# A memset between row scatters: GpSimd clears a spare tile after each indirect DMA

## The chip, the cores and the metric

The kernel runs on one core of one Trainium2 chip. The metric is the device time of one execution in microseconds (us), as the median over timed runs. The profile of one separate execution, taken by the hardware profiler, gives what the engines did and when.

## The reference

The input is `hidden`, 16 sequences of 512 rows of 256 numbers (8192 rows). Layer one is a memory network trained at test time; layer two is a top-1 mixture of 8 experts.

```
k, v, q = dwconv4(h @ Wk.T), dwconv4(h @ Wv.T), dwconv4(h @ Wq.T)     # 64 columns each
alpha, eta, theta = mean(sigmoid/sigmoid/softplus of h @ aW.T, h @ eW.T, h @ tW.T)
for chunk of 128 rows:
    g = clip(grad of sum((silu(k W1.T) W2.T - v)^2) at the chunk's first W)   # per row
    scan over rows: Sm = eta Sm - theta g;  W = (1 - alpha) W + Sm
    retrieved = silu(q W1.T) W2.T          # with each row's own W
out = rmsnorm(retrieved @ Wo.T) * norm_g * (h @ gW.T + gb)
x = layernorm(h + out)
e = argmax(x @ gate_w.T)                   # one of 8 experts for each row
result = layernorm(x + x @ expert_w[e].T)
```

## The kernel before, in words

The 16 sequences are split into 4 groups (g) of 4, and the 512 rows into 4 chunks (c) of 128, which makes 16 steps (c, g) of layer one. Each step goes through `project`, `respond`, `learn`, `retrieve` and `epilogue`. These are Python generators: each `yield` ends a piece, and the string `ORDER`, written out by hand, says in which order the pieces' instructions are put on the engines' queues. An engine runs its own queue strictly in order; between engines, semaphores decide (`mark` counts an instruction, `wait` waits for a count).

The end of `epilogue` sends the rows of layer one to DRAM, sorted by expert. It computes for each row its place (`where_f`, then `index`, an int32 cast on GpSimd), and then GpSimd issues four indirect DMAs (L1033), one for each sequence of the group: each writes 128 rows of 260 numbers to 128 places of `sorted_rows`. That is 64 scatters in all. They read `rows`, which has two buffers.

The second layer is `experts()`. It works on 36 pairs of tiles of 128 sorted rows (the last pair has one tile, so 71 tiles). For pair t: `load` (SP issues two row loads from `sorted_rows`), `turn` (TensorE transposes, ScalarE copies, L1228), `multiply` (eight TensorE matmuls, L1248, then statistics on VectorE, L1252 to L1261), `scale` (the layernorm's factors, ACT L1267 and DVE L1269 and L1271), `send` (ScalarE writes the normalized rows to `os`, two instructions of L1282; GpSimd scatters them to `out`, one indirect DMA a tile, L1287). There are six load buffers, three transposed ones and four `os` buffers, so `send(t)` on ScalarE waits until the scatter of pair t-4 has landed. Which tile belongs to which expert is worked out by `table` in three parts; the first part needs the scatters of steps 0 to 11, so the expert pairs run partly beside the last four steps of layer one, and the pairs of the last table need all 64 scatters.

What else GpSimd does, in the same queue: small operations of the epilogue (L931, L933 for `rms`, L955 to L960 for `rstd`), of `learn` (L797 to L803, `weight` L812), the loads of the residual (L943), `end_c` (L705), `routed` (L1021) and, in the first 13 steps, wide products (L699, L715, L809, L850). The constructs at L98 (`M.apart`) add one to a semaphore on an engine's sequencer to keep two waits apart.

At the end SP waits until the last scatters have landed (L1307). The program ends there.

Of the kernel before, what the change touches and what calls it, by code (L numbers as in the profile page):

```python
# [27 lines left out]
P = 128  # L28
B = 16
S = 512  # L30
H = 256
# [37 lines left out]
class Counts:  # L69
# [9 lines left out]
    def mark(self, e, name, instruction):  # L79
        instruction.then_inc(self.sem[e], 1)  # L80
        self.count[e] += 1
        self.at[name] = (e, self.count[e])

    def wait(self, e, *names):

        need = {}
        for name in names:
            if int(name.rsplit(".", 1)[1]) >= 0:
                who, n = self.at[name]
                need[who] = max(need.get(who, n), n)  # L90
        for who, n in need.items():
            if self.reached[e, who] < n:
                self.engines[e].wait_ge(self.sem[who], n)
                self.reached[e, who] = n
# [54 lines left out]
def build(nc, dram):  # L149
    out = dram["out"]  # L150
    with ExitStack() as ctx:
# [193 lines left out]
        nc.vector.wait_ge(s_prep, n_bias)  # L345

        layers(nc, ctx, sb, sem, dict(locals()))


def layers(nc, ctx, sb, sem, v):  # L350
# [12 lines left out]
    pe, act, dve, pool, sp = nc.tensor, nc.scalar, nc.vector, nc.gpsimd, nc.sync  # L363
# [3 lines left out]
    def two(name, shape, dt=F32):  # L367
        return [sb(f"{name}{i}", shape, dt) for i in range(2)]
# [65 lines left out]
    where_f = sb("where_f", [P, NB])  # L434
    index = two("index", [P, NB], I32)
    s_scatter = [sem(f"s_scatter{i}") for i in range(2)]

    pro = Slots("pro", banks[0:3], NC * G * 9 + NC * G // 2)
    lrn = Slots("lrn", banks[3:4], NC * G * 4)
# [471 lines left out]
    def epilogue(c, g):  # L911
# [120 lines left out]
        for b in range(NB):  # L1032
            pool.indirect_dma_start(sorted_rows[:, :], bass.IndirectOffsetOnAxis(index[i2][:, b:b + 1], 0), R[:, b, :], None,  # L1033
                                    bounds_check=NE * REGION - 1, oob_is_err=False).then_inc(s_scatter[i2], 16)
        yield

    s_blank = sem("s_blank")
# [144 lines left out]
    def tiles_of(t):  # L1182

        return 1 if t == PAIRS - 1 else 2
# [5 lines left out]
    def moved(t):  # L1190

        return 32 * (t // LOADS) + 16 * tiles_of(t)
# [80 lines left out]
    def send(t):  # L1273

        o = t % ROWS_OUT
        key, both = product[t]
        if t >= ROWS_OUT:
            act.wait_ge(s_out[(t - ROWS_OUT) % LOADS], moved(t - ROWS_OUT))
        wait("act", f"x_shift.{t}")
        for i in range(tiles_of(t)):  # L1280
            mark("act", f"x_os{i}.{t}" if i < tiles_of(t) - 1 else f"x_os.{t}",
                 act.activation(os_[o][:, i, :], both[:, i, :], ACT.Identity, bias=rs[o][:, 2, i:i + 1], scale=rs[o][:, 1, i:i + 1]))  # L1282
        late.freed_by(key, f"x_os.{t}")
        for i in range(tiles_of(t)):
            wait("pool", f"x_os{i}.{t}" if i < tiles_of(t) - 1 else f"x_os.{t}", f"x_tok.{t}")
            M.apart("pool")
            pool.indirect_dma_start(out[:, :], bass.IndirectOffsetOnAxis(xs_token[t % LOADS][:, i:i + 1], 0), os_[o][:, i, :], None,  # L1287
                                    bounds_check=TOK - 1, oob_is_err=False).then_inc(s_out[t % LOADS], 16)

    def experts():  # L1290

        for t in range(PAIRS + 2):
            for stage, lag in ((load, 0), (turn, 0), (scale, 2), (multiply, 1), (send, 2)):
                if 0 <= t - lag < PAIRS:
                    stage(t - lag)
                    yield
# [3 lines left out]
    for letter, stage in dict(p=project, s=respond, l=learn, r=retrieve, e=epilogue).items():  # L1300
        steps.update({f"{letter}{n:x}": stage(n // G, n % G) for n in range(NC * G)})
# [74 lines left out]
```

## Time and profile before

| what | value |
|---|---|
| median of 3 runs | 544.11 us (542.71 to 547.35) |
| the profiled execution: span from first to last instruction | 578.0 us (no other time of this execution is given) |
| TensorE busy | 458.5 us, 79% |
| VectorE busy | 376.7 us, 65% |
| GpSimd busy | 326.8 us, 57% |
| ScalarE busy | 309.7 us, 54% |
| TensorE clock granted, mean | 0.910 of full |

The profiled execution is the longest of the executions told of here: its span is 33.9 us over the median of the timed runs. All rows below are of that execution. Busy shares are averages over stages with different limits. On the page, "L1287" is line 1287 of the kernel; "issue" is idle time in which no wait is visible, and "remote" or "another core or an unknown queue" a wait that ended with a semaphore event for which the profile names no instruction.

### The profile page before, as it was taken

The numbers are of one execution on the slowest core, as the hardware profiler recorded it, in microseconds if no ns is written. First come the engines' busy times: TensorE is split into PE (matmuls) and PEld (weight loads), VectorE is DVE, ScalarE is ACT, GpSimd is POOL, SyncE is SP. The second block draws the span as 40 slices with busy tenths as digits, with TensorE's granted clock in tenths as the row PEclk, the third lists the DMA queues.
The fourth block names the chain that finished last, engine by engine and source line by source line (L and its number), as shares of the span: only waits on it lengthen the run. The fifth ranks groups of instructions, "written<-read, shape, count | busy, mean of one in ns | idle before, by whom it ended". The sixth has DMA issues, their size and how long they took to land.

```text
span 578.0 us, 11149 instructions
## 1 busy us (share of the span) xinstructions
PE 458.5 (79%) x3502; PEld 347.1 (60%) x3502; DVE 376.7 (65%) x1123; ACT 309.7 (54%) x779; POOL 326.8 (57%) x451
## 2 busy tenths in 40 slices
PE   4589889999888998888998898766858774855773
PEld 2356656777665877667675775555646553644662
DVE  3365886898795868769789696777644543333433
ACT  1254375566575485665738656464656553314544
POOL 2004535446748686685757657672477666445466
PEclk9797999999998999998999999885887987768788
DMA  8412352345553536445263545474364644425431
GB/s 228 130 74 61 107 124 71 120 129 101 158 130 96 161 85 164 95 141 135 79 176 74 157 110 151 134 231 110 93 178 133 177 140 137 131 91 161 130 120 43
DMA packets 61354, 73.21 MB, mean 127 GB/s; under 512 B 17293, under 2 KB 48206, under 8 KB 61296
## 3 DMA queue, kind: packets, MB, share of 16 engines
q1 hardware_dynamic: 50624, 46.12, 28.5%
q0 software_dynamic: 8848, 25.44, 16.6%
q10 hardware_dynamic: 1824, 0.93, 0.6%
q8 instruction: 29, 0.48, 0.4%
q14 instruction: 29, 0.24, 0.2%
HBM read 44.19 MB, written 19.22 MB: 110 GB/s over the span
## 4 chain that ended last, share of the span: by engine, by line
PE 41%; DVE 20%; ACT 11%; issue 10%; POOL 8%; another core or an unknown queue 5%; DMA 3%; SPq 1%; ACTq 0%; POOLq 0%; DVEq 0%
DVE kq_in L559 8%; PE bank L518 6%; PE bank L1248 5%; PE bank L605 4%; POOL sorted_rows L1033 3%; PE bank L536 3%; ACT rows L966 2%; PE bank L920 2%; PE both L1248 2%; ACT os L1282 2%; PE bank L686 2%; DVE gt L609 1%; PE both L886 1%; PE bank L1225 1%
## 5 line engine op out<-in xcount | busy, mean ns | idle before, releaser
L1287 POOL DMA_INDIRECT out<-os,xs_token x71 | 70.1, 988 | 46.0 <-ACT os L1282 26.4
L1033 POOL DMA_INDIRECT sorted_rows<-rows,index x64 | 68.7, 1074 | 30.0 <-issue 16.6
L1248 PE MATMUL bank<-shared,front 128*128 x212 | 60.6, 435 | 27.3 <-ACT rs L1267 8.5
L518 PE MATMUL bank<-front 128*64 128x256 f32 x512 | 64.8, 408 | 13.3 <-DMA bias_t<-in_bias_t 7.7
L559 DVE SCALAR_TENSOR_TENSOR kq_in<-shared,conv_w,kq_in 128x256 f32<-128x256 f32 x144 | 69.0, 536 | 9.5 <-ACT kq_in L553 9.3
L605 PE MATMUL bank<-front 128*128 128x256 f32 x256 | 63.1, 396 | 4.8 <-DVE bias_g L324 4.8
L1248 PEld LDWEIGHTS bank<-shared,front 128*128 128x128 f32 x212 | 43.9, 219 | 36.5 <-issue 30.3
L518 PEld LDWEIGHTS bank<-front 128*64 128x64 f32 x512 | 38.8, 148 | 34.4 <-issue 10.8
L605 PEld LDWEIGHTS bank<-front 128*128 128x128 f32 x256 | 48.2, 196 | 12.7 <-issue 6.6
L937 DVE SCALAR_TENSOR_TENSOR y<-bank,rms,gt 128x256 f32<-128x256 f32 x64 | 26.5, 476 | 17.1 <-POOL rms L933 10.2
L1252 DVE BATCH_NORM_STATS2 st<-bank 128x6 f32<-128x256 f32 x53 | 20.2, 421 | 26.3 <-remote 11.9
L927 ACT ACTIVATE junk<-bank 128x256 f32<-128x256 f32 x64 | 24.6, 384 | 22.7 <-PE bank L920 10.2
L966 ACT ACTIVATE rows<-y,rstd 128x256 f32<-128x256 f32 x64 | 33.2, 595 | 5.6 <-POOL rstd L960 3.3
L1228 ACT ACTIVATE front<-bank 128x512 f32<-128x512 f32 x28 | 16.7, 596 | 35.7 <-remote 24.8
L1282 ACT ACTIVATE os<-bank,rs 128x256 f32<-128x256 f32 x53 | 27.0, 560 | 15.2 <-DVE rs L1271 12.2
L536 PE MATMUL bank<-front 128*128 128x512 f32 x64 | 31.6, 617 | 0.0
L609 DVE TENSOR_TENSOR gt<-bank,bias_g 128x512 f32<-128x512 f32 x32 | 21.2, 680 | 10.8 <-PE bank L605 10.7
L1248 PE MATMUL both<-shared,front 128*128 x72 | 22.9, 474 | 5.7 <-ACT front L1228 4.7
L850 POOL TENSOR_TENSOR ab_h<-hq,carry 128x512 f32<-128x512 f32 x13 | 17.4, 1340 | 14.8 <-DMA hq<-hq 14.8
L553 ACT ACTIVATE kq_in<-shared,conv_b,conv_w 128x256 f32<-128x256 f32 x48 | 25.3, 595 | 0.8 <-PE bank L686 0.8
L948 DVE BATCH_NORM_STATS2 stats<-y 128x6 f32<-128x256 f32 x64 | 22.4, 411 | 3.5 <-DMA y<-in_hidden 3.5
L793 DVE TENSOR_REDUCE norms<-sq 128x16 f32<-128x1024 f32 x16 | 19.5, 1216 | 7.3 <-ACT sq L790 5.6
(212 smaller groups left out, 1185.3 us busy)
## 6 DMA issues: line engine op xcount, KB each, us to landing
front<-sorted_rows SPq DMA_DIRECT2D x71, 130.0 KB
front<-in_hidden_t SPq DMA_DIRECT2D x16, 512.0 KB
decay<-gate_clear SPq DMA_DIRECT2D x16, 512.0 KB
y<-in_hidden POOLq DMA_DIRECT2D x16, 512.0 KB
q<-kq_in SPq DMA_DIRECT2D x64, 64.0 KB, 2.1
carry<-carry_rows SPq DMA_DIRECT2D x32, 128.0 KB, 2.8
hq<-hq SPq DMA_DIRECT2D x64, 64.0 KB
shared<-in_w_expert SPq DMA_DIRECT2D x2, 1024.0 KB
```

Source lines behind the costliest of these rows:

```text
L518: ins = pe.matmul(halves[half(side), kind, :, :], w[:, k, kind * D:(kind + 1) * D], pairs[:, k, side, :, :], start=k == 0, stop=k == KH - 1)
L536: ins = pe.matmul(bank[:, :], w_ae[:, k, :], xt[:, k, :], start=k == 0, stop=k == KH - 1)
L553: act.activation(kq_in[i2][:, kind, :, :], raw[g][:, kind, :, 0:P], ACT.Identity, bias=conv_b[:, kind:kind + 1], scale=conv_w[:, kind, 0:1]))
L559: dve.scalar_tensor_tensor(dst, raw[g][:, kind, :, tap:tap + P], conv_w[:, kind, tap:tap + 1], dst, ALU.mult, ALU.add))
L605: ins = pe.matmul(bank[:, (b % 2) * H:(b % 2 + 1) * H], xt[:, k, b * P:(b + 1) * P], w_g[:, k, :], start=k == 0, stop=k == KH - 1)
L609: mark("dve", n(f"gt{two_of}"), dve.tensor_tensor(gt[g][:, 2 * two_of:2 * two_of + 2, :], bank[:, :].rearrange("p (b f) -> p b f", b=2), s ...
L937: mark("dve", n(f"gated{b}"), dve.scalar_tensor_tensor(Y[:, b, :], wo[b], rms[:, 1, b:b + 1], gt[g][:, b, 0:H], ALU.mult, ALU.mult))
L966: act.activation(R[:, b, 0:H], Y[:, b, :], ACT.Identity, bias=rstd[:, 2, b:b + 1], scale=rstd[:, 1, b:b + 1])
L1033: pool.indirect_dma_start(sorted_rows[:, :], bass.IndirectOffsetOnAxis(index[i2][:, b:b + 1], 0), R[:, b, :], None, bounds_check=NE * REGI ...
L1248: ins = pe.matmul(both[:, i, :], xs_t[t % TURNED][:, i, k, :], w_expert[:, k, bass.ds(expert, 1), :], start=k == 0, stop=k == KH - 1)
L1282: act.activation(os_[o][:, i, :], both[:, i, :], ACT.Identity, bias=rs[o][:, 2, i:i + 1], scale=rs[o][:, 1, i:i + 1]))
L1287: pool.indirect_dma_start(out[:, :], bass.IndirectOffsetOnAxis(xs_token[t % LOADS][:, i:i + 1], 0), os_[o][:, i, :], None, bounds_check=TO ...
```

## The change

A spare tile of 128 x 256 float32 and a semaphore are added. After each indirect DMA, in `epilogue` (64) and in `send` (71), GpSimd clears the spare tile (a memset), which adds one to the semaphore. From the second memset on, GpSimd first waits until the memset before it is done. Nothing waits for the landing of a scatter that did not wait before. No instruction is removed.

```diff
     s_scatter = [sem(f"s_scatter{i}") for i in range(2)]
+    spare = sb("spare", [P, H])
+    s_apart = sem("s_apart")
+    cleared = [0]
+
+    def keep_apart():
+
+        if cleared[0]:
+            pool.wait_ge(s_apart, cleared[0])
+        pool.memset(spare[:, :], 0.0).then_inc(s_apart, 1)
+        cleared[0] += 1
...
         for b in range(NB):
             pool.indirect_dma_start(sorted_rows[:, :], ... R[:, b, :] ...).then_inc(s_scatter[i2], 16)
+            keep_apart()
...
             pool.indirect_dma_start(out[:, :], ... os_[o][:, i, :] ...).then_inc(s_out[t % LOADS], 16)
+            keep_apart()
```

## Rows read from the trace of the kernel before

**Rows 1.** The page's head, engines and the chain by engine.

```profile
span 578.0 us, 11149 instructions
...
PE 458.5 (79%) x3502; PEld 347.1 (60%) x3502; DVE 376.7 (65%) x1123; ACT 309.7 (54%) x779; POOL 326.8 (57%) x451
...
POOL 2004535446748686685757657672477666445466
...
DMA  8412352345553536445263545474364644425431
...
PE 41%; DVE 20%; ACT 11%; issue 10%; POOL 8%; another core or an unknown queue 5%; DMA 3%; SPq 1%; ACTq 0%; POOLq 0%; DVEq 0%
```

**Rows 2.** Timeline of POOL, the last scatters: start, us, what, idle before.

```profile
565.65 0.97 POOL L1287 DMA_INDIRECT out<-os,xs_token  x1 [3.87 <-ACT os L1282]
...
574.59 0.97 POOL L1287 DMA_INDIRECT out<-os,xs_token  x1 [0.31 <-issue]
575.87 0.97 POOL L1287 DMA_INDIRECT out<-os,xs_token  x1 [0.30 <-issue]
```

**Rows 3.** Timeline, 418 to 426 us.

```profile
418.72 1.89 PE L1248 MATMUL bank<-shared,front 128*128 x8
...
419.95 1.02 POOL L1287 DMA_INDIRECT out<-os,xs_token  x1 [0.30 <-issue]
...
420.97 0.27 POOL L1021 TENSOR_TENSOR routed<-routed,onehot 128x32 bf16<-128x32 bf16 x1
...
421.41 1.01 POOL L1287 DMA_INDIRECT out<-os,xs_token  x1 [0.17 <-issue]
...
422.72 0.97 POOL L1287 DMA_INDIRECT out<-os,xs_token  x1 [0.30 <-issue]
```

**Rows 4.** Groups by line, engine POOL, whole span.

```profile
L1287 POOL DMA_INDIRECT out<-os,xs_token x71 | 70.1, 988 | 46.0 <-ACT os L1282 26.4 <-issue 16.4 <-DVE st L1252 1.8
L1033 POOL DMA_INDIRECT sorted_rows<-rows,index x64 | 68.7, 1074 | 30.0 <-issue 16.6 <-POOL index L1029 12.8 <-ACT sq L783 0.3
...
L290 POOL TENSOR_SCALAR_AFFINE_SELECT ident_nb<-ident_nb 128x512 f32<-128x512 f32 x1 | 0.6, 630 | 0.0
...
L290 POOL TENSOR_SCALAR_AFFINE_SELECT ident<-ident 128x128 f32<-128x128 f32 x1 | 0.3, 282 | 7.4 <-DVE coef L278 7.4
...
L1039 POOL MEMSET rows<- 128x16 f32 x2 | 0.2, 111 | 0.1
...
L1371 POOL MEMSET const-float32-1.0<- 128x1 f32 x1 | 0.1, 98 | 0.0
```

**Rows 5.** The chain that ended last, 520 to 560 us.

```profile
by line: another core or an unknown queue 34.9%; PE bank L1248 18.9%; ACT os L1282 15.3%; issue 10.0%; ACT front L1228 9.6%; PE both L1248 5.3%; PE bank L1225 3.3%; ACT rs L1267 3.1%; DVE rs L1271 1.7%; PE both L1225 1.7%; DVE rs L1269 1.5%
...
524.65 1.02 ACT os L1282 x2
...
526.82 1.02 ACT os L1282 x2
527.84 5.55 another core or an unknown queue
...
534.34 3.78 PE bank L1248 x8
```

**Rows 6.** Timeline, 509 to 517 us.

```profile
508.75 2.64 PE L1248 MATMUL bank<-shared,front 128*128 x6
...
511.23 0.60 PE L1225 MATMUL bank<-ident,front 128*128 128x128 f32 x4
512.36 0.97 POOL L1287 DMA_INDIRECT out<-os,xs_token  x1 [0.30 <-issue]
515.56 0.76 DVE L1252 BATCH_NORM_STATS2 st<-bank 128x6 f32<-128x256 f32 x2 [8.12 <-remote]
515.62 0.60 ACT L1228 ACTIVATE front<-both 128x512 f32<-128x512 f32 x1 [7.06 <-remote]
...
516.57 0.17 DVE L1261 CAST xs_token<-front 128x2 int32<-128x2 f32 x1
```

**Rows 7.** Who waited for whom, whole span: us, times, longest.

```profile
ACT front L1228 <- remote: 31.8, 7, 7.1
...
DVE st L1252 <- remote: 23.6, 5, 8.1
```

**Rows 8.** The chain that ended last, by line, whole span.

```profile
by line: issue 9.9%; DVE kq_in L559 8.0%; PE bank L518 6.3%; PE bank L1248 5.4%; another core or an unknown queue 4.8%; PE bank L605 3.5%; POOL sorted_rows L1033 3.4%; PE bank L536 3.0%; ACT rows L966 2.5%; PE bank L920 2.1%; PE both L1248 
```

**Rows 9.** Timeline of POOL, 220 to 232 us.

```profile
226.47 1.08 POOL L1033 DMA_INDIRECT sorted_rows<-rows,index  x1 [0.30 <-issue]
227.63 0.60 POOL L955 TENSOR_SCALAR rstd<-mv 128x4 f32<-128x4 f32 x1
228.31 0.23 POOL L956 TENSOR_SCALAR rstd<-mv 128x4 f32<-128x4 f32 x1
228.51 1.04 POOL L958 TENSOR_TENSOR rstd<-rstd,minus_half 128x4 f32<-128x4 f32 x1
```

**Rows 10.** Groups by line, 500 to 578 us.

```profile
L1287 POOL DMA_INDIRECT out<-os,xs_token x41 | 39.9, 973 | 33.9 <-ACT os L1282 21.6 <-issue 10.1 <-DVE st L1252 1.8
```

**Rows 11.** DMA issues of 500 to 578 us.

```profile
out<-os,xs_token POOLq DMA_INDIRECT x41
...
sorted_rows<-rows,index POOLq DMA_INDIRECT x3
```

**Rows 12.** POOL busy by stretch: us, busy (instructions), clock, DMA share.

```profile
core 0: us, POOL busy (x), PEclk, DMA share, GB/s
0.00:416.00 416.00, 232.36 (x343) 0.95 0.48 126
416.00:503.00 87.00, 54.46 (x67) 0.82 0.50 146
503.00:578.00 75.00, 39.99 (x42) 0.80 0.35 110
```

**Rows 13.** Timeline of POOL, 498 to 504 us.

```profile
499.58 0.98 POOL L1033 DMA_INDIRECT sorted_rows<-rows,index  x1 [0.30 <-issue]
...
503.42 0.97 POOL L1287 DMA_INDIRECT out<-os,xs_token  x1 [0.31 <-issue]
```

## The prediction

> **What bounds the kernel now.** I read the page's head first, then the chain of waits, then GpSimd's timeline, because the change touches only GpSimd. The head [rows 1] shows no engine at its limit over the whole span: TensorE 79%, GpSimd 57%. GpSimd's row of tenths shows where that mean misleads: the late slices are not its fullest, yet the last thing to run in the whole program is GpSimd scattering rows [rows 2]. The chain names no one owner: VectorE's convolution (8.0%), TensorE's projections (6.3%), and 3.4% for the scatters of L1033 [rows 8]. So before the tail GpSimd counts only where something is queued behind a scatter.
>
> In the tail it is different. Scatters that are ready follow each other every 1.28 us (574.59 to 575.87), 0.97 of it in the span and 0.30 between, also where nothing else is waited for [rows 2]. A pair has two, so GpSimd wants 2.56 us a pair. ScalarE, undisturbed, goes from one pair's `os` to the next in 2.17 us (524.65 to 526.82) [rows 5]. GpSimd is therefore the slower of the two, and a backlog of scatters builds up. But in this profiled execution it also sits idle for 33.9 us in front of the 41 last output scatters, 21.6 of it for ScalarE [rows 10]. Why ScalarE is late is the odd part: TensorE's transposes are over at 511.83, and VectorE and ScalarE, both of which need only TensorE, start together at 515.56 and 515.62, after 8.12 and 7.06 us of waiting that the profile gives to "remote" [rows 6]. GpSimd's burst of scatters ended at 513.33. The same shape returns at 527.84, where the chain has 5.55 us of it [rows 5]. Over the span the chain has 4.8% of it, 27.7 us [rows 8], and the two largest waits of this kind add to 55.4 us on two engines that wait side by side [rows 7]. TensorE's signals come late while GpSimd makes descriptors.
>
> The important choice of this prediction is what to do with these stalls. The profiled span is 578.0 us and the timed median 544.11, so timed runs lack 33.9 us (by chance the figure of GpSimd's idle time above), and the stalls are 27.7 us on the chain plus the slow restart of TensorE behind each (3.78 us for eight matmuls [rows 5] instead of 1.89 [rows 3]). I take it that the timed runs have little of them. Then a timed tail is one of GpSimd at its own pace: the 44 last scatters (41 of L1287 and 3 of L1033 [rows 11]) would take 44 x 1.28 = 56 us, where in the profile they take 77 us (from 499.58 [rows 13] to 575.87 + 0.97 [rows 2]). That gives back 21 of the 33.9 us that timed runs lack.
>
> **The change, part by part.** It removes and moves nothing. It adds 135 memsets and 134 waits.
>
> *The wait.* Each memset waits for the memset before it. Between them there is at least a scatter of 0.97 us on the same in-order queue, so the wait is met when it is reached. Behind it in the queue stand only GpSimd's own operations. I cost it at nothing; if it were not met in time it would cost a semaphore's passage, some 0.08 us, as between two small operations of `rstd` (227.63 + 0.60 to 228.31 [rows 9]).
>
> *The memset.* The trace has no memset of this size on GpSimd. One column takes 98 ns and sixteen 111 ns [rows 4]: 0.87 ns a column, so 256 columns 98 + 255 x 0.87 = 320 ns. The other one-input operation, affine_select, takes 282 ns for 128 columns and 630 for 512 [rows 4]: 0.91 a column and 398 ns for 256. Bounds are the 111 ns row below and the 630 ns row above. I take 0.32, the line of the same operation.
>
> *What it adds to the scatter's period.* Part of the memset can hide in the 0.30 us between two scatters. The trace has one such case: `routed` (0.27 us) starts the moment a scatter ends, and the next scatter starts 0.17 us after it, so 419.95 to 421.41 is 1.46 us instead of 1.28 [rows 3]. A memset of 0.32 makes it 0.97 + 0.32 + 0.17 = 1.46, that is 0.185 more; with the 0.398 of affine_select 0.26, with 0.63 0.50, with 0.11 nothing. I round the likely value to 0.2 us.
>
> *The tail.* 44 scatters x 0.2 = 8.8 us, all on the path, if GpSimd sets the pace there. It has the margin already: 2.56 us a pair against ScalarE's 2.17 [rows 5], and 2.96 afterwards. The very last memset runs beside the landing of the last scatter and costs nothing.
>
> *Everything before the tail.* 91 scatters (61 of L1033, 30 of L1287) x 0.2 = 18.2 us of GpSimd time, spread over a queue that is 56% busy up to 416 us and 63% from 416 to 503 [rows 12]. What of it reaches the path? Of the 68.7 us of L1033's scatters [rows 4] the chain has 3.4% of 578, 19.7 us [rows 8], 29%: the operations behind a group of four scatters (`rstd` at 228.51 after the burst that ended at 227.55 [rows 9]) are sometimes what ScalarE and VectorE need next. With the same share, 0.29 x 18.2 = 5.3 us.
>
> *The other engines.* The memset writes SBUF 135 times for 0.32 us, and VectorE works at the same time. The Trainium skill (SBUF — State Buffer, Who interferes with whom) speaks against the change here: VectorE and GpSimd share a port pair, which a VectorE copy, cast or tensor_scalar can hold for its whole length, and then a memset waits, or the other way round; an operation that reads two inputs only meets GpSimd's reads, and a memset has none. By that rule the cost is at most the short casts of the tail (0.17 us, at 516.57 [rows 6], for one), which the rows do not show meeting anything, and it stays out of the sum.
>
> **Sum.** 8.8 + 5.3 = 14.1 us. On the profiled execution's 578.0 that would be 592 if its stalls stayed as they are; on the timed median, 544.1 + 14.1 = 558 us. The stalls of the profiled execution can hide part of it, so I expect the profile after to show less than 14 more.
>
> **Rivals.**
>
> *A, the tail isn't GpSimd's in timed runs either.* If TensorE at the lower clock (3.78 us for a pair's matmuls, [rows 5]) or the stalls set the pace, the added time disappears in GpSimd's idle 33.9 us [rows 10]. Then all 135 x 0.2 = 27 us count with 29%, 7.8 us, giving 552. For it: that idle time. Against it: the 33.9 us that timed runs lack.
>
> *B, the memset hides altogether.* If a scatter keeps only part of GpSimd busy and the memset's work fits in the 0.30 us between two spans, the period stays near 1.28 and the time at 544 to 547. Against it: the 0.27 us of `routed` did lengthen it by 0.19 [rows 3]. The Trainium skill has a rule that would lead there (Perfetto Trace Analysis, DMA Instruction — SWDGE (GPSIMD)): two of the engine's processors make the descriptors, and the span ends when the last of them has written its last one, before its program ends. By it six of the eight could clear their part early; the rows do not separate them.
>
> *C, faster: the spacing lets TensorE's signals through.* Bursts of back-to-back scatters end in waits of 4 to 8 us on ScalarE and VectorE [rows 6]. If the cause is that descriptor making leaves no room, and if timed runs have these stalls too, a pause of 0.5 us in each 1.5 could dissolve them. It would take away up to the chain's 27.7 us and cost the 14.1: 530.5 us. It decides from the point where more than 14 of the 27.7 us are real in timed runs and go away. For it: the stalls line up with the bursts. Against it: the 33.9 us between profile and median, and that one pause of 0.44 us (420.97 to 421.41, [rows 3]) left the next scatter at its usual 1.01 us, a sign that nothing was pent up on GpSimd's own side.
>
> *D, the change doesn't do what it says.* The memset may run before the scatter's descriptors are made or beside them; then it separates nothing. Its time is B's.
>
> **How the numbers follow.** My forecast (GpSimd sets the tail, memset 0.3 to 0.4 us) has 50%: from 0.12 us of added period with 29% of it before the tail (5.3 + 3.2 us) to 0.26 with 60% (11.4 + 14.2 us), 552 to 570 us. A has 18%: 547 to 556. B and D together 15%: 542 to 549. C has 17%: 520 to 540. Faster or slower than 1% (5.4 us, about what a measurement of this kernel tells from no change) means below 538.7 or above 549.6. Slower: 50 and most of A's 18 make 64%. Same: the rest of A, B and a part of C, 21%. Faster: 15%. The range of 8 in 10 leaves out most of C below and the worst memset above (0.50 x 44 = 22 and 0.50 x 91 x 0.29 = 13, 579 us): 539 to 572.
>
> **What will show it in the profile after.** Memset: a group of 135 at 0.3 to 0.4 us with GpSimd's busy time up by about 43 us. Period: 1.46 us between scatters of a burst. Tail: in the last 50 us GpSimd without idle time, if the stalls are gone there. C right: the "remote" waits of L1228 and L1252 shrink from 55.4 us to under half. B right: period under 1.33. The prediction is wrong if the memset takes over 0.6 us, if the timed tail isn't GpSimd's, or if the timed runs do have the stalls that I take for the profiled execution's own.

## The result, and the profile after

The changed kernel took 576.26 us (median, 573.5 to 579.23), the kernel before 544.11 (542.71 to 547.35): 1.057 times, interval 1.0491 to 1.0648. It is 32 us slower, where 14 were forecast.

The page of the changed kernel, its head, engines, GpSimd's row of tenths and the chain by engine and line:

```profile
span 574.7 us, 11284 instructions
...
PE 454.9 (79%) x3502; PEld 343.8 (60%) x3502; DVE 381.3 (66%) x1123; ACT 309.4 (54%) x779; POOL 369.2 (64%) x586
...
POOL 2004535536848595758577585678538888878888
...
PE 27%; DVE 23%; POOL 23%; ACT 11%; issue 7%; DMA 6%; SPq 1%; POOLq 1%; ACTq 0%; DVEq 0%
DVE kq_in L570 9%; POOL sorted_rows L1044 8%; PE bank L529 5%; POOL out L1299 4%; POOL spare L445 4%; ACT rows L977 3%; PE bank L547 3%; DMA out<-os,xs_token 3%; PE bank L616 2%; POOL rstd L969 2%; ACT os L1294 2%; PE bank L1260 2%; PE bank L931 2%; PE both L897 2%; DVE gt L620 1%
```

GpSimd is busy 42.4 us longer than in [rows 1] (326.8), has gone from 8% of the chain to 23% (12% in before_again_2 below, a profile of the kernel before that fits its timed runs), and is 80% or more busy in nine of the last ten slices. The span, though, is 3.3 us *shorter* than the 578.0 of [rows 1], while the timed median is 32 us longer: profile and times of the kernel before do not belong together, and the experiments had to find out why. The groups of GpSimd, and two of the last three scatters:

```profile
L1044 POOL DMA_INDIRECT sorted_rows<-rows,index x64 | 72.0, 1125 | 23.4 <-POOL index L1040 13.7 <-issue 9.2 <-ACT w_t L918 0.2
L1299 POOL DMA_INDIRECT out<-os,xs_token x71 | 70.2, 989 | 13.0 <-issue 7.4 <-ACT os L1294 1.5 <-DVE mvs L1269 0.8
L445 POOL MEMSET spare<- 128x256 f32 x135 | 45.3, 336 | 0.1
```

```profile
569.73 0.97 POOL L1299 DMA_INDIRECT out<-os,xs_token  x1 [0.16 <-issue]
570.69 0.33 POOL L445 MEMSET spare<- 128x256 f32 x1
571.19 0.97 POOL L1299 DMA_INDIRECT out<-os,xs_token  x1 [0.17 <-issue]
```

The memset takes 0.336 us, starts the moment the scatter ends, and the next scatter starts 0.17 us after it: a period of 1.46 us (569.73 to 571.19) against 1.28 in [rows 2]. Its idle time of 0.1 us for 135 says that the new wait never held it. The idle time in front of the output scatters is down from 46.0 us [rows 4] to 13.0 (before_again_2 has 21.7, nearly all of it the 0.30 us in front of each of 71, so the change itself took off only some 9), and no wait on "remote", of which [rows 7] had 55.4 us, is left among the waits of this profile.

### The profile page after: what moved, and what is told of

The parts are those of the page before. It is cut to its first block, busy times and chain, and to the rows that moved or that the text cites. A ratio compares the mean times of both kernels' runs of the same rounds, so it can differ in the third digit from the quotient of the medians.

```text
span 574.7 us, 11284 instructions
## 1 busy us (share of the span) xinstructions
PE 454.9 (79%) x3502; PEld 343.8 (60%) x3502; DVE 381.3 (66%) x1123; ACT 309.4 (54%) x779; POOL 369.2 (64%) x586
## 3 DMA queue, kind: packets, MB, share of 16 engines
q0 software_dynamic: 8848, 25.44, 16.9%
## 4 chain that ended last, share of the span: by engine, by line
PE 27%; DVE 23%; POOL 23%; ACT 11%; issue 7%; DMA 6%; SPq 1%; POOLq 1%; ACTq 0%; DVEq 0%
DVE kq_in L570 9%; POOL sorted_rows L1044 8%; PE bank L529 5%; POOL out L1299 4%; POOL spare L445 4%; ACT rows L977 3%; PE bank L547 3%; DMA out<-os,xs_token 3%; PE bank L616 2%; POOL rstd L969 2%; ACT os L1294 2%; PE bank L1260 2%; PE bank L931 2%; PE both L897 2%; DVE gt L620 1%
## 5 line engine op out<-in xcount | busy, mean ns | idle before, releaser
L1044 POOL DMA_INDIRECT sorted_rows<-rows,index x64 | 72.0, 1125 | 23.4 <-POOL index L1040 13.7
L1260 PE MATMUL bank<-shared,front 128*128 x212 | 54.5, 402 | 11.8 <-ACT rs L1279 6.7
L1260 PEld LDWEIGHTS bank<-shared,front 128*128 128x128 f32 x212 | 40.3, 200 | 19.2 <-issue 14.3
L445 POOL MEMSET spare<- 128x256 f32 x135 | 45.3, 336 | 0.1
L547 PE MATMUL bank<-front 128*128 128x512 f32 x64 | 34.0, 656 | 5.6 <-ACT k_n L658 3.5
L984 PE MATMUL bank<-ident,rows 128*128 128x128 f32 x128 | 21.1, 319 | 14.7 <-DVE y L948 12.9
L984 PEld LDWEIGHTS bank<-ident,rows 128*128 128x128 f32 x128 | 17.3, 165 | 17.8 <-DVE y L948 14.4
L1032 POOL TENSOR_TENSOR routed<-routed,onehot 128x32 bf16<-128x32 bf16 x16 | 7.7, 479 | 31.4 <-PE bank L1029 15.3
L804 DVE TENSOR_REDUCE norms<-sq 128x16 f32<-128x1024 f32 x16 | 19.5, 1217 | 12.1 <-ACT sq L801 12.0
L861 POOL TENSOR_TENSOR ab_h<-hq,carry 128x512 f32<-128x512 f32 x13 | 18.2, 1401 | 14.1 <-DMA hq<-hq 14.1
```

Of the source, the lines that this page charges most:

```text
L445: pool.memset(spare[:, :], 0.0).then_inc(s_apart, 1)
L547: ins = pe.matmul(bank[:, :], w_ae[:, k, :], xt[:, k, :], start=k == 0, stop=k == KH - 1)
L984: ins = pe.transpose(bank[:, b * P:(b + 1) * P], R[:, b, k * P:(k + 1) * P], ident[:, :])
L1260: ins = pe.matmul(both[:, i, :], xs_t[t % TURNED][:, i, k, :], w_expert[:, k, bass.ds(expert, 1), :], start=k == 0, stop=k == KH - 1)
```

## The experiments

### Two kinds of chip

The kernel before, unchanged (again, before_again_2), and the changed kernel, unchanged (changed_again, changed_3, changed_4), each beside timed runs of the kernel before on the same chip.

> The kernel before, unchanged, as a second look at its profile. The timed time should be 543 to 547 us. Theory 1 (the profiled execution shown before was disturbed: the late TensorE signals belong to it and not to the timed runs) expects this profile's span either again near 578 with the remote waits of L1228 and L1252 (profiling brings them on each time) or near 543 without them (they come by chance). Theory 2 (the stalls are in every execution) would need a timed time near 578, and has been contradicted by the median of 544 already.

It took 576.68 us, and the kernel before beside it 576.92 (0.9988, interval 0.9956 to 1.0019) on one chip. The two largest waits on "remote" in its profile:

```profile
ACT front L1228 <- remote: 33.8, 6, 12.0
DVE st L1252 <- remote: 18.7, 4, 6.8
```

The profiled execution took 577.06 us, as long as the timed runs. So what [rows 6, 7] show, waits of ScalarE and VectorE for TensorE that end late (I call it "late signals"; the profile names no instruction for their end), is not made by profiling.

> The kernel before, for its profile beside the others of this job. If its time is 577, late signals (remote waits of some 50 us) should be in the profile, by both theories; if it is 544, none, and the last 44 scatters should follow each other at 1.28 us with little idle time, ending near 541.

On the next chip it took 544.14 us (kernel before beside it: 547.14). Its page, and the end of its timeline:

```profile
span 545.8 us, 11149 instructions
...
PE 450.9 (83%) x3502; PEld 340.9 (62%) x3502; DVE 380.8 (70%) x1123; ACT 309.0 (57%) x779; POOL 324.9 (60%) x451
...
POOL 2004346274674958647666848476716777667777
...
PE 34%; DVE 25%; POOL 12%; DMA 10%; ACT 9%; issue 8%; SPq 1%; ACTq 0%; POOLq 0%; DVEq 0%
```

```profile
541.11 0.97 POOL L1287 DMA_INDIRECT out<-os,xs_token  x1 [0.30 <-issue]
542.38 0.97 POOL L1287 DMA_INDIRECT out<-os,xs_token  x1 [0.31 <-issue]
543.66 0.97 POOL L1287 DMA_INDIRECT out<-os,xs_token  x1 [0.30 <-issue]
```

Its waits have no "remote" at all. Same program, same durations of scatters, same period of 1.28 us, and 32 us less span than in [rows 1]. The five chips of these experiments are of two kinds, which I call "prompt" (the kernel before at 546 and 547 us: two chips) and "late" (574 to 579 us: three); the times of the result, with the kernel before at 544, are those of a prompt chip. By span and waits the profile from which the prediction was made is of the late kind, and the times beside it are of the prompt kind; on which chips they were taken is not known. Each of the five chips was met in one job only, so whether the kind stays with a chip or changes with time is not shown either; within a job it did not change.

> The changed kernel, unchanged, timed alternately with the kernel before on one chip. The kernel before took 577 us in the last job where it had taken 544 before, so two conditions of the chip have to be told apart: one in which TensorE's signals come late during bursts of scatters (profile before, and the last job), one in which they do not. Theory 1 (the change costs its 32 us wherever it runs) expects 577 + 32 = 609 us beside 577. Theory 2 (in the condition with late signals the memsets also take the lateness away) expects the same or less than before: 560 to 580 beside 577. Both expect 576 beside 544 if the chip is in the other condition now.

On the prompt chip: 574.3 us beside 547.14, ratio 1.0511 (1.0444 to 1.0579).

> The changed kernel once more. If the kernel before takes 577 here: the sum of the two parts measured on such chips (output memsets -11, layer one's +3) expects about 570 us; a cost that is the same wherever it runs (27 to 32 us) expects 604 to 609. If before takes 545: 574 as before.

Another prompt chip: 570.56 beside 546.07, ratio 1.0455 (1.037 to 1.054).

> The changed kernel. Where before takes 577: about 570 if the parts measured on such chips add (output memsets -8 to -11, layer one's +3); 602 to 604 if the 25 to 27 us of cost come on top wherever it runs. Where before takes 545: 571 to 574 again.

A late chip: 575.69 beside 574.46, ratio 0.9993 (0.9944 to 1.0043). Neither number of the expectations was met exactly, but the cost of 25 us on top is excluded: the changed kernel takes 571 to 576 us everywhere, and what differs between chips is the kernel before. The profile of changed_4 shows where the cost went. Its two largest groups of waits on "remote":

```profile
DVE st L1264 <- remote: 11.3, 6, 3.3
ACT front L1240 <- remote: 4.9, 4, 2.1
```

That is 16.2 us against 52.5 in again, and nothing of it is left in the chain (0% against 8%). The 41 last output scatters follow each other in 61.7 us (514.60 to 576.28) instead of 70.6.

### Which memsets cost: output scatters or layer one's

```diff
             pool.indirect_dma_start(sorted_rows[:, :], ...)
-            keep_apart()                # send_only, send_only_2, send_only_3
...
             pool.indirect_dma_start(out[:, :], ...)
-            keep_apart()                # epilogue_only, _2, _3
```

> The memsets only after the 71 output scatters (L1287). Theory 1 (each memset adds its 0.19 us of GpSimd time, and that counts where GpSimd sets the pace) expects 71 x 0.19 = 13.5 us at most, 41 x 0.19 = 8 us at least: 552 to 558. Theory 2 (the memset breaks a pipelining of back-to-back scatters that timed runs have, so that each costs more than 0.19) expects about 71 of 135 parts of the 32 us or more: 561 to 570.

> The memsets only after the 64 scatters of layer one (L1033). Theory 1 (0.19 us each, 29% of it on the path) expects 64 x 0.19 x 0.29 = 3.5 us, at most all 12 us: 547 to 556. Theory 2 (more than 0.19 each) expects 10 to 20 us: 554 to 564. Together with the run with the output memsets alone the two differences should add to 32 us if the costs are independent.

Both were written for a prompt chip and met a late one: 565.6 and 580.37 beside 576.92, ratios 0.9797 (0.9748 to 0.9847) and 1.0065 (1.0 to 1.013). Memsets after output scatters made the kernel *faster* there, by 1.5% to 2.5%. In the profiles of that chip the 31st output scatter, the first of the last 41, and the last one stand like this, without memsets (again) and with output memsets (send_only):

```profile
503.12 0.97 POOL L1287 DMA_INDIRECT out<-os,xs_token  x1 [0.31 <-issue]
...
573.74 0.97 POOL L1287 DMA_INDIRECT out<-os,xs_token  x1 [0.30 <-issue]
```

```profile
500.23 0.97 POOL L1298 DMA_INDIRECT out<-os,xs_token  x1 [0.30 <-issue]
...
564.33 0.97 POOL L1298 DMA_INDIRECT out<-os,xs_token  x1 [0.17 <-issue]
```

From 70.6 us to 64.1, although each period is 0.19 longer. The waits on "remote" of ScalarE's L1228 and VectorE's L1252 went from 52.5 us to 32.0:

```profile
ACT front L1239 <- remote: 17.4, 6, 8.0
DVE st L1263 <- remote: 14.6, 6, 6.2
```

> Memsets only after the 71 output scatters, as before; the first time was on a chip with late signals, where it was 2% faster. If this chip has none: Theory 1 (everything that GpSimd adds is on the path, 0.19 us for each scatter) expects +13.5 us over the kernel before; Theory 2 (the tail's 41 in full, the 30 before with the 29% of the prediction) +9.4 us. If this chip has late signals: 8 to 12 us faster than before once more.

> Memsets only after the 64 scatters of layer one. On a chip without late signals Theory 1 (all of it on the path) expects 16 groups x (3 x 0.19 + 0.34) = 14.6 us over before; Theory 2 (29% of it) 4.2 us. With late signals: 0 to 6 us over before, as the first time.

A late chip again, and again faster with output memsets: 571.18 and 582.24 beside 579.21, ratios 0.9857 (0.9785 to 0.993) and 1.005 (1.0008 to 1.0091).

> Memsets only after the 71 output scatters. Where before takes 545: +13.5 us if all of GpSimd's added time is on the path, +9.4 with 29% of it ahead of the tail. Where before takes 577: -8 to -12 us.

> Memsets only after the 64 scatters of layer one. Where before takes 545: +14.6 us if all is on the path, +4.2 with 29%. Where before takes 577: +3.

Prompt at last: 559.71 and 557.2 beside 546.07, ratios 1.0212 (1.0125 to 1.0299) and 1.0214 (1.0133 to 1.0295), 11.6 and 11.7 us. Together 4.3%, where the same chip gave 4.55% for both at once: within the intervals the two costs add. For the output memsets the interval is 7 to 16 us and holds both theories' numbers, 13.5 and 9.4; for layer one's it is 7 to 16 too, which holds 14.6 and excludes 4.2. That run is the one that tells full length from 29%.

### Length or interruption

```diff
-        pool.memset(spare[:, :], 0.0).then_inc(s_apart, 1)
+        pool.memset(spare[:, 0:1], 0.0).then_inc(s_apart, 1)      # one_column, _2, _3
```

> All 135 memsets, but of 1 column (0.10 us) instead of 256. Theory 1 (GpSimd's time) expects a period of 0.97 + 0.10 + 0.17 = 1.24 us, not longer than the 1.28 of before, and so no cost: 542 to 547. Theory 2 (it is the interruption that costs, not its length) expects most of the 32 us to stay: 560 to 576.

> All 135 memsets, of one column. The first profile has 1.28 us between scatters of a burst with them (0.97 + 0.13 + 0.19), the period of before. On a chip without late signals Theory 1 (only the time that GpSimd loses counts) expects 0 to 3 us over before (16 + 71 x 0 between, 0.13 behind a group's last). A theory by which the semaphore or the interruption itself costs would give 20 us or more.

> All 135 memsets, of one column. Where before takes 545: 0 to 3 us over before if only GpSimd's lost time counts, 20 or more if the interruption or its semaphore costs. Where before takes 577: +3 us.

On late chips 1.0067 (1.0014 to 1.0119) and 1.0055 (1.0009 to 1.0101), on the prompt one 547.77 beside 546.07, ratio 1.0016 (0.9967 to 1.0065). Its timeline on the prompt chip:

```profile
530.96 0.97 POOL L1299 DMA_INDIRECT out<-os,xs_token  x1 [0.19 <-issue]
531.92 0.12 POOL L445 MEMSET spare<- 128x1 f32 x1
532.24 0.97 POOL L1299 DMA_INDIRECT out<-os,xs_token  x1 [0.19 <-ACT front L1240]
```

All 135 memsets, waits and increments are there, the period is the old 1.28 us, and nothing is lost that the interval (-1.8 to 3.6 us) would show. So semaphore and interruption are not what cost 25 to 32 us; the length of the memset beyond the 0.13 us that hide between two scatters is. On the late chips it gave no gain in time, and the 41 last output scatters stayed at 72.2 and 70.3 us.

The other direction, `spare` with 512 columns, after output scatters alone:

> Memsets of 512 columns instead of 256, after the 71 output scatters alone. Each is 0.22 us longer, 0.55 in all. Theory 1 (length counts, nothing is gained by the pause): 41 x 0.22 = 9 us or more over the run with 256 columns there. Theory 2 (the pause relieves TensorE's signals, and a longer one more): the same or less than that run's ratio of 0.98 to before.

On a prompt chip 570.67 beside 547.14, ratio 1.0453 (1.0384 to 1.0521). With 256 columns it was 1.0212, on the other prompt chip: 0.22 us more for each of 71 scatters, 15.6 us, cost some 13 (2.41% of 546). That is what Theory 1's rule gives, GpSimd's added length in full. Theory 2 was about late signals, which a prompt chip has none of, so whether a longer pause relieves them more was not tried.

### Between the four, or behind the last

```diff
+            if b < NB - 1:              # between_three; b == NB - 1: behind_last, _2
                 keep_apart()
```

In these runs the memsets after output scatters are taken out as well.

> Memsets only between the four scatters of a group in layer one (48 instead of 64, none behind the fourth, none after output scatters). With all 64 the last job's profile had the thirteenth group start at 437.9 us instead of 424.8, some 1.1 us a group. Theory 1 (each memset adds 0.19 us between two scatters and its whole 0.34 behind the last) expects 0.57 us a group, the thirteenth group 7 us late: 430 to 433. Theory 2 (what costs is anything that GpSimd does between scatters) expects three quarters of the delay: 435.

On a prompt chip 552.52 beside 547.14, ratio 1.0138 (1.0064 to 1.0211), 7.5 us (3.5 to 11.5) for 48 memsets of which each adds 0.19: 9.1. That excludes 29% of it (2.6), but doesn't tell Theory 1 from Theory 2, whose shares of the 11.7 us for all 64 (7.3 and 8.8) are too near each other. The place where I looked for it misled: the thirteenth group starts at 427.3 us, 426.3 in before_again_2, and in that pair of profiles the loss showed only after that. The expectation of 430 to 433 rested on profiles of late chips.

> One memset a group of layer one, behind its fourth scatter, and none elsewhere (16 in all); the complement of the run with memsets between the four. On a chip without late signals Theory 1 (GpSimd's time) expects 16 x 0.34 = 5.4 us, Theory 2 1.6 us, and Theory 3 (a delay of the rstd operations right behind a group upsets the hand-written order more than its own length) 8 us or more.

> One memset a group of layer one, behind its fourth scatter (16 in all). Where before takes 545: +5.4 us if each costs its own 0.34 us, 8 us or more if keeping rstd waiting upsets the order more than that; 11.7 less 7.5 us, that is 4, if it is the complement of the runs with 64 and with 48 memsets in layer one. Where before takes 577: 0 to 2 us over before.

Both met late chips: 579.8 beside 579.21, ratio 1.0017 (0.998 to 1.0054), and 575.6 beside 574.46, 1.0019 (0.9967 to 1.007). No upset by a delayed `rstd` shows there; on a prompt chip it wasn't tried, and the 4 us that are left of 11.7 for 64 memsets after 7.5 for 48 are an inference, near the 16 x 0.34 = 5.4.

## Why the prediction was wrong

**The memset, 0.32 us: right.** Measured 0.336. **The period, 1.46 us: right,** as `routed` in [rows 3] had shown. **The wait, nothing: right,** by its idle time of 0.1 us and by the run with one column.

**The tail, 8.8 us: right.** On one prompt chip, the first scatter of the twelfth group, the 31st output scatter and the last, in before_again_2 and in changed_again:

```profile
388.32 1.10 POOL L1033 DMA_INDIRECT sorted_rows<-rows,index  x1 [0.90 <-POOL index L1029]
...
492.56 0.97 POOL L1287 DMA_INDIRECT out<-os,xs_token  x1 [0.30 <-ACT os L1282]
...
543.66 0.97 POOL L1287 DMA_INDIRECT out<-os,xs_token  x1 [0.30 <-issue]
```

```profile
397.37 1.10 POOL L1044 DMA_INDIRECT sorted_rows<-rows,index  x1 [0.90 <-POOL index L1040]
...
512.02 0.97 POOL L1299 DMA_INDIRECT out<-os,xs_token  x1 [0.17 <-issue]
...
570.65 0.97 POOL L1299 DMA_INDIRECT out<-os,xs_token  x1 [0.17 <-issue]
```

The tail goes from 51.1 to 58.6 us, 7.5 more for 40 periods (0.19 each). GpSimd does set its pace on a prompt chip, as forecast from the missing 33.9 us.

**Everything before the tail, 5.3 us: this step failed.** It is the term "with the same share, 0.29 x 18.2 = 5.3 us". In the same pair of profiles the tail starts 19.5 us later (492.56 to 512.02), 9.1 of them already at the twelfth group. That is all of the 18.2 us, not 29% of it. Single profiles scatter here: changed_3 starts its tail at 508.9 us and the profile of the result at 514.0, so the delay is 16 to 21 us.

The timed runs say the same. With the measured prices GpSimd's added time, all of it counted, is 71 x 0.19 + 16 x (3 x 0.19 + 0.34) = 28 us. The three comparisons with the kernel before at 544 to 547 us gave, by their ratios, 31, 28 and 25 us; all three intervals (27 to 35, 24 to 32, 20 to 30) hold 28 and none holds the forecast 14.1. The two parts (11.6 + 11.7) give 23, less than 28 but within their intervals. The 18.2 itself was a little small: behind the fourth scatter of a group the whole 0.34 us is paid, not 0.2, which is 2 us for 15 groups.

How the delay gets through is seen in who waits for GpSimd's small operations of `rstd` and `rms`, which stand behind the scatters in its queue. First before_again_2, then changed_again:

```profile
DVE y L937 <- POOL rms L933: 10.7, 4, 3.7
ACT rows L966 <- POOL rstd L960: 9.3, 5, 3.2
```

```profile
ACT rows L977 <- POOL rstd L971: 28.4, 10, 5.1
DVE y L948 <- POOL rms L944: 19.6, 5, 7.7
```

From 20.0 us to 48.0. The 29% was the share of the scatters' *present* time that one chain through a profile of the late kind happened to run through. A chain tells which instruction ended a wait now; it does not tell which ones will when the engine gets later in every group. In the chain of the result's profile the scatters of L1044 have 8.0%, where L1033 has 3.4% in [rows 8] and 4.1% in before_again_2, and the memsets themselves 4% of 574.7, 23 us, half of their 45.3. That GpSimd was only 56% busy up to 416 us [rows 12] was no protection. My reading is that its idle time lies where it waits for data that its own earlier work had made late; the waits above fit that, but no run isolates it.

TensorE's clock is not the cause: changed_3 was granted 0.925 and before_again_2 0.926, and TensorE was busy 447.7 and 450.9 us, with spans of 569.5 and 545.8.

**The stalls: half right.** That the timed runs of the result lack them was right, and so was the sign against rival C. But "the profiled execution's own" was wrong: on three chips the timed runs of the kernel before have their cost. **Rival C** is what happens there in part: memsets after output scatters gain 1.4% to 2%, and the full change comes out even. Its sign, "remote" waits of L1228 and L1252 under half of 55.4 us, is met in changed_4 (16.2 us). Beside behind_last_2, a profile of the same chip with 16 memsets and no cost in time, the tail of changed_4 starts 12.7 us later (501.89 to 514.60) and is 6.5 us shorter (68.2 to 61.7), where on the prompt chip it started 19.5 us later and was 7.5 us longer. So a relief of some 21 us stands against the cost in these two profiles. By the timed medians it is some 25 us, since the profiled execution of changed_4 took 579.6 us, 3.9 over its median. Both are estimates from differences. The two parts, as measured on each of the other late chips (-2.0% and +0.6%, -1.4% and +0.5%), add to about 1% faster, and the full change was even on the third. C does not turn the sign of the full change; it does turn that of the output memsets alone. **Rival A** (the tail isn't GpSimd's) describes the tail of the kernel before on a late chip, 70.6 us instead of 51.1. **B and D** are out: the memset runs after the scatter's span and adds to its period.

**Open.** Why TensorE's signals are late during bursts on some chips is not settled. Of the profiles of the late kind, the three with 0.50 us between the spans of output scatters (0.17 + 0.33) have the shortest tails, 61.7 to 64.1 us. The six with 0.30 us there have 68.2 to 72.5, and the two with 0.32 us 72.2 and 70.3. The sum of the waits on "remote" tells less: with 0.32 us it was 47.5 us on the two lines in one profile and 16.9 in another. Prompt chips show nothing of it with the same program. The profile of the result cannot tell whether the memsets took late signals away, since the kernel before has none on such a chip; changed_4 says that they took away most.

No version beat the kernel before on a prompt chip. On late chips the kernel with output memsets alone was the fastest.

## What to carry to other kernels

Price an addition to an in-order engine that serves every iteration of a loop at its full length times its count, and take off only what a named row shows to be idle behind it in every iteration. The engine's share of the chain was no discount here (29% forecast, all of it paid). Set a profile's span beside the timed median of the same kernel: where they differ as here (34 us), rows of the profile may describe another condition than the times, and a change has to be compared on one chip in one job. Between two scatters a little fits for nothing (0.13 us), and what is longer is paid in part (0.19 of 0.34 us was).

## What the runs showed of the hardware

This kernel took 546 and 547 us on two chips and 574, 577 and 579 on three, while the granted clock is near the same (0.926 in before_again_2, 0.909 in again). What sets the profiles apart is the time that ScalarE and VectorE wait on "remote", where the rows show only TensorE's work in front of them, around GpSimd's bursts of indirect DMAs: 52.5 us in the two largest groups of waits in again, none in before_again_2. On GpSimd, a memset of 128 x 256 float32 takes 0.336 us, one of 512 columns 0.55, one of a single column 0.13 us when it follows a scatter (0.098 before the first one [rows 4]), and the gap in front of the next scatter shrinks from 0.30 to 0.17 or 0.19 us when a memset or `routed` stands between them.
